# One group of turns moved behind another in the tile loop of a Metaformer block

## What is computed

```python
# x: (4, 512, 16, 32)
x = x + conv_ref(ln_c(x), w3, w7, w15, w_mix)   # three causal depthwise convolutions, mixed
t = to_tokens(x)                                # 2048 tokens of 512 numbers
# ffn_ref(ln_t(t)): 8 experts, the best 2 for each token, softmax weights
h = silu(einsum('nf,efh->enh', xn, w1)) * einsum('nf,efh->enh', xn, w3)   # hidden 1024
y = einsum('enh,ehf->enf', h, w2)
out = t + einsum('enf,ne->nf', y, full_w)
```

## Time and profile before

| | us |
|---|---|
| median of 3 runs | 848.08 (847.98 to 848.32) |
| span of the profiled execution | 845.4 |
| PE busy in it | 791.5 (94%) |
| DVE busy | 351.7 (42%) |
| ACT busy | 318.6 (38%) |
| POOL busy | 268.8 (32%) |

### The profile page before, as it was taken

The page is one execution under the profiler, slowest core; times in us unless marked ns, Lnnn a source line. Parts: engine busy times, 40 slices in busy tenths (PEclk is TensorE's granted clock), DMA queues, the critical chain, the costliest instruction groups (busy, mean ns, idle before and its releaser), DMA issues.

```text
span 845.4 us, 13004 instructions
## 1 busy us (share of the span) xinstructions
PE 791.5 (94%) x3764; PEld 655.6 (78%) x3765; DVE 351.7 (42%) x791; ACT 318.6 (38%) x487; POOL 268.8 (32%) x313
## 2 busy tenths in 40 slices
PE   4999999628999999999999999999999999999993
PEld 3777888527888888888888888888888888888882
DVE  5886758685113621172216223511361172244111
ACT  6784755432214512262127125311441262262120
POOL 4346210003233422361216315322341262243311
PEclk9999999659999999999999999999999999999997
DMA  7247678628111811173116513712281164111111
GB/s 237 47 75 138 150 162 175 256 105 326 25 31 34 317 39 25 27 263 95 32 30 201 159 25 88 271 25 37 46 302 37 25 224 136 25 37 25 30 32 25
DMA packets 55873, 91.72 MB, mean 108 GB/s; under 512 B 7344, under 2 KB 40496, under 8 KB 49712
## 3 DMA queue, kind: packets, MB, share of 16 engines
q1 hardware_dynamic: 45728, 71.64, 27.2%
q0 software_dynamic: 9408, 19.42, 12.0%
q10 hardware_dynamic: 720, 0.46, 0.2%
HBM read 64.97 MB, written 18.15 MB: 98 GB/s over the span
## 4 chain that ended last, share of the span: by engine, by line
PE 86%; DVE 7%; DMA 2%; issue 2%; ACT 1%; POOL 0%; POOLq 0%; ACTq 0%; DVEq 0%
PE bank L720 23%; PE bank L718 23%; PE bank L719 23%; PE bank L734 4%; PE bank L631 3%; PE bank L632 3%; PE bank L633 3%; PE bank L712 2%; PE bank L653 1%; DMA xg<-xn_rows,gather_at 1%; DVE bn L782 1%; DVE wc_lo L823 1%; PE bank L671 1%; PE bank L646 1%; DVE mv L791 1%
## 5 line engine op out<-in xcount | busy, mean ns | idle before, releaser
L718 PE MATMUL bank<-w_hi,xT_hi 128*128 128x512 f32 x576 | 229.0, 398 | 4.3 <-DVE xT_lo L1019 4.3
L720 PE MATMUL bank<-w_hi,xT_lo 128*128 128x512 f32 x576 | 225.9, 392 | 0.0
L719 PE MATMUL bank<-w_lo,xT_hi 128*128 128x512 f32 x576 | 225.2, 391 | 0.0
L1042 DVE TENSOR_TENSOR h<-bank,h 128x512 f32<-128x512 f32 x72 | 49.8, 692 | 294.0 <-PE bank L720 293.8
L718 PEld LDWEIGHTS bank<-w_hi,xT_hi 128*128 128x128 f32 x576 | 108.9, 189 | 26.3 <-DVE xT_lo L1019 4.7
L720 PEld LDWEIGHTS bank<-w_hi,xT_lo 128*128 128x128 f32 x576 | 108.7, 189 | 23.4
L719 PEld LDWEIGHTS bank<-w_lo,xT_hi 128*128 128x128 f32 x576 | 108.9, 189 | 21.8
L718 PE MATMUL bank<-w_hi,hT_hi 128*128 128x512 f32 x288 | 118.7, 412 | 0.0
L559 ACT ACTIVATE h<-bank 128x512 f32<-128x512 f32 x72 | 43.1, 599 | 197.4 <-PE bank L720 197.4
L720 PE MATMUL bank<-w_hi,hT_lo 128*128 128x512 f32 x288 | 112.6, 391 | 0.0
L719 PE MATMUL bank<-w_lo,hT_hi 128*128 128x512 f32 x288 | 112.3, 390 | 0.0
(11 more groups left out here) (145 smaller groups left out, 924.2 us busy)
## 6 DMA issues: line engine op xcount, KB each, us to landing
w_raw<-in_units SPq DMA_DIRECT2D x48, 1024.0 KB, 5.9
joint<-xs_parts SPq DMA_DIRECT2D x64, 128.0 KB, 3.8
out_x<-XT SPq DMA_DIRECT2D x17, 256.0 KB, 3.6
XT<-in_x SPq DMA_DIRECT2D x16, 256.0 KB, 7.0
xn_rows<-xnb SPq DMA_DIRECT2D x16, 256.0 KB, 2.5
xg<-xn_rows,gather_at POOLq DMA_INDIRECT x37, 3.4
out_x<-y,add_at POOLq DMA_INDIRECT x36
gate_row<-gate_rows,gate_at POOLq DMA_INDIRECT x36
```

Of the source, the lines that this page charges most:

```text
L718: pe.matmul(B[bank][:], stat_hi, hi, start=start, stop=False)
L719: pe.matmul(B[bank][:], stat_hi, lo, start=False, stop=False)
L720: return pe.matmul(B[bank][:], stat_lo, hi, start=False, stop=stop)
L1042: dve.tensor_tensor(h[:, j, :], B[2 * j + 1][:], h[:, j, :], ALU.mult).then_inc(h_out, 1)
```

## The change

Four lists change. On TensorE, `turn_tokens(t + 2)` moves from behind `up(3)` to directly behind `turn_h(1)`, and `turn_h(1)` comes after two products of `down(0)` instead of one. The order is now `up(3)`, two products, `turn_h(1)`, `turn_tokens`, two products, `down(1)`. On ACT, the copy `hi(1)` comes ahead of the copy into `xT_hi`, and on DVE `rest_of_hT(1)` comes ahead of `xT_rest`. On POOL, ahead of tile 0, the gather of tile 1's rows comes ahead of the wait for the stored gates and of the gather of tile 0's gates. No instruction is added or taken away.

```diff
             pool.wait_ge(tables_ready, 1)
+            pool.tensor_copy(gather_at[:], src_i[:, bass.ds(column(1), 1)]).then_inc(gather_index, 1)
+            pool.wait_ge(xg_ps, 1)
+            pool.wait_ge(gather_index, 1)
+            gather(gather_at[:, 0:1])
             pool.wait_ge(gate_st, 16)
             gather_gates(gate_i[:, 0:1])
-            pool.wait_ge(xg_ps, 1)
-            pool.tensor_copy(gather_at[:], src_i[:, bass.ds(column(1), 1)]).then_inc(gather_index, 1)
-            pool.wait_ge(gather_index, 1)
-            gather(gather_at[:, 0:1])
...
                 silu(1)
                 hi(0)
                 next_expert(2)
+                hi(1)
                 act.wait_ge(xg_ps, t + 2)
                 act.activation(xT_hi[:], B[6][:].rearrange("p (q i) -> p q i", i=P),
                                ACT.Copy).then_inc(xT_hi_out, 1)
-                hi(1)
...
                 up(3)
-                turn_tokens(t + 2)
                 pe.wait_ge(lo_ready[4], split)
                 pe.wait_ge(hT_lo_out, t * 2 + 1)
                 if not isinstance(t, int):
                     pe.wait_ge(y_out, t)
-                down(0, (0,))
+                down(0, (0, 1))
                 turn_h(1)
-                down(0, (1, 2, 3)).then_inc(unit_done, 1)
+                turn_tokens(t + 2)
+                down(0, (2, 3)).then_inc(unit_done, 1)
...
                 gate_up(1)
+                rest_of_hT(1)
                 xT_rest(t + 2)
-                rest_of_hT(1)
```

## The result

The changed kernel took **843.08 us** (median of 5 runs, 842.65 to 844.94) against 848.06 us before (5 runs, 847.32 to 848.32): ratio 0.9948, 95% interval 0.9937 to 0.9959. That is 5.0 us faster. The direction was forecast, the size was not: the prediction said 2.8 us, 845.3, and its range ended at 844.3. In a second set the same two programs stood at 0.9958 (0.9943 to 0.9972), 3.6 us.

What follows compares the result with a forecast made beforehand. TensorE, busy throughout the loop, was taken to bound the kernel, with one wait in tile 0. Terms of -2.39 us (tile 0) and -0.4 us (two groups) gave -2.8 us, from 848.08 to 845.3 us, range 844.3 to 847.2.

Steps and rivals of the forecast that it cites:

- What bounds the kernel, and where it loses time: TensorE is full in the loop; its gap is in tile 0, 2.39 us waiting for the gather of tile 1's rows.
- Two groups in place of three: TensorE's turns in each tile: merging two groups saves a tail, -0.01 us a tile, -0.4 over 36 tiles.
- the tails: Extra 0.02 to 0.05 us behind each group of turns; rival: doubled behind eight turns, +1.1 us, 846.8, chance 0.07.
- hT_lo, the tight place: Before down(1): hT_lo ends 1.35 us behind h's turns, cover 1.83, no cost; rival wait there, chance 0.09.
- the spare of 0.15 us: At down(1): how late its load may start without loss, 0.05 us plus lateness already seen behind turns.
- The turned rows, POOL, the expert changes: Loop: rows turned 1.83 us later, 2 us remain; POOL queues nothing; seven expert changes keep 0.6 us; no cost.
- The clock behind eight turns: Rival in each tile: clock falls behind the double group, losing 3.3 us a tile, about 963 us; chance 0.01.
- The gather in tile 0: Tile 1's rows gathered from 188.1 us, landing by 196.5: gain 2.39 us, or 1.83 if landing as before.
- not held: Rival before tile 0: gather held until DVE's low halves end, gain 1.83 instead of 2.39 us, 845.9; chance 0.07.
- the last line of the sum: Whole kernel: -2.39 - 0.4 = -2.8 us; span 845.4 to 842.6, median, 2.7 us longer, 848.08 to 845.3.
- the term for tile 0: TensorE's wait in tile 0 for the gather of tile 1's rows, taken away whole: -2.39 us.

Runs made afterwards that it cites:

- the two traces of 620.91 and 620.90 us: Loop times of the changed kernel (843.08 us) and of the kernel before with only the TensorE, ACT and DVE lists changed (845.11 us).
- the other two: Changed kernel once more, 843.90 us; changed kernel with the low half of tile 0's rows first on DVE, 841.54 us.
- The two runs with less cover: Changed kernel with three products ahead of the turns and one behind, 866.38 us; changed kernel with the old order on ACT and DVE, 878.47 us.

## Why the prediction was right or wrong

- *What bounds the kernel, and where it loses time*: right. The only gap that the change could close was the wait in tile 0, and 2.60 of the 3.6 us between the two spans are there; 1.1 are in the first part.
- *Two groups in place of three*: -0.4 us was forecast, within bounds of -0.7 to +1.1. Measured is nothing in the two traces of 620.91 and 620.90 us, and -0.8 and -0.9 in the other two. In the first trace the tails stay wherever the groups stand (17.74 us in a tile against 17.75). The bound of -0.7 was passed by a little in those two. That the forecast lies between the two kinds of execution is luck.
- *hT_lo, the tight place*: right, by 0.01 us (1.35, and 1.82 for 1.83). The two runs with less cover waited 0.61 and 0.95 us in each tile, where 0.54 to 0.64 and 0.95 to 1.05 were reckoned. Of the spare of 0.15 us the wake takes 0.07 more than I had counted, so some 0.08 are left.
- *The turned rows, POOL, the expert changes*: right in the sum. No tile of the loop is longer than before, those where the expert changes included.
- *The clock behind eight turns*: the granted clock is 1.00 from 208 to 829 us of the first trace, so that rival did not come.
- *The gather in tile 0*: right in place. It starts at 187.72 (reckoned 188.1), but against the tables it is 0.7 us later than reckoned, 3.54 us behind them and not 2.82; that the two times nearly agree is luck. It was not held: its issue took 0.97 us, and the gather of the gates was the slow one (2.61). With some 3.6 us from issue to landing it had long landed when TensorE came to the turns, so none of this cost anything. If it had come as late as before, 0.56 us should have been lost. In the run with POOL's old list tile 0 is 0.77 longer (31.36 against 30.59), but 0.45 of it lie ahead of the wait: the last matmul of up(3) began 24.24 us behind the indices there, and 23.79 in the changed kernel. Some 0.3 are left for the wait.
- **The step that failed is the last line of the sum, with the size of the term for tile 0**, 2.39 us. I took one profiled execution as the typical one, and put the 2.7 us between its span and the median down to what lies around the span. A run's time is 1.62 to 1.74 us above its own span. So that execution would have taken some 847.05 us, while the median before was 848.06: 1.0 of the 2.7 was time spent inside the program by the runs of the median. The 5.0 us then come apart so: 1.0 by which the profiled execution before was short, 3.6 between the two spans (2.60 in tile 0, 1.1 in the first part, -0.1 behind the loop), and 0.4 by which the profiled execution after was long (843.52 against 843.08).
- What the term for tile 0 left out is shown in part. Another execution of the kernel before lost 2.44 us more at the same wait: 0.80 from its later end and 1.64 behind it, where the clock fell to 1.2 GHz. Against that one the change gains 5.0 us in tile 0, against the short one 2.6. Nearly all runs of the kernel before above 848.7 us in the later sets have the lower granted clock too (14 of 15), and no run of the changed kernel has it (0.969 to 0.971). Whether the runs of the first set, at 847.32 to 848.32 between the two groups, lost their 1.0 us there or in the first part is not known: their clock is not on record.
- The prediction had the clock among its rivals, but at the wrong place: behind the eight turns of the changed kernel, where it never fell. It named the idle 203 to 205 us with the clock at 1.00 as evidence against a fall, and did not ask what a wait one us longer would do. The Trainium skill, "TensorE: Matmul & The Clock Gate", section "Why this matters for your kernels", advises against idle gaps of TensorE between bursts of matmuls. The traces agree with it: behind 2.2 us idle the clock stayed, behind 3.2 and 4.7 us it fell. A range that took this in would have had its lower end some 2 us deeper.

## What to carry to other kernels

Before a sum starts from one profiled execution, set its span beside the spread of the runs. If the difference between span and median is more than a run's time is above its own span (here 1.7 us), some executions lose time that this trace does not show; a wait is one place to look, and the part that the change does not touch is another. A single idle stretch of TensorE has two prices, its length and the clock behind it, and the second comes and goes with small shifts. Where two groups of short work are merged on a full engine, count on little (here 0 to 0.9 us in 35 tiles), and check what cover the merging takes from the chain behind it.

## What the runs showed of the hardware

- The granted clock fell to 0.50 behind 3.2 us and behind 4.7 us of idle TensorE, and stayed at 1.00 behind 2.2 us. The stretch at 0.50 was 3.4 us long in the first case; in the second it began before the turns did and ended at about 212. It cost 1.6 and 2.7 us.
- A load that waits for two semaphores started 0.12 us behind the later one (0.114 to 0.117 in 36 tiles), one that waits for one 0.05.
- POOL's small copies and gathers ran late beside DVE's low halves: the copy of the indices took 1.42 to 1.79 us where it takes 0.18 elsewhere, the gathers 2.5 to 3.1 instead of 1.0. Whether the gather of the gates or that of the rows was caught differed from execution to execution of the kernel before; the wait ended 0.8 us later where it was that of the gates.
